# The order of two places in VectorE's program, in a fused GroupNorm, Hadamard and MLP kernel

## The reference

```python
# cut to what matters
x = x + L0(gn(x))      # L0: along the channels, pad 192 -> 256, times a 256 x 256 Hadamard matrix / 16, keep 192
x = x + L1(gn(x), ...) # L1: at each position, over its 192 channels:
#   h = x @ W1.T + b1
#   h = gelu(layernorm(h, g1, beta1))
#   h = h @ W2.T + b2
#   h = gelu(layernorm(h, g2, beta2))
#   h = h @ W3.T + b3
# gn: over 32 groups of 6 channels, mean and variance over the group's channels and all positions of an image
```

## Time and profile before

| | before |
|---|---|
| median of 3 runs | 938.48 us |
| lowest, highest | 937.85, 939.48 us |
| the profiled execution | 939.39 us |
| its span in the trace | 937.6 us |
| busy: PE, DVE, ACT, POOL | 91%, 90%, 86%, 60% of the span |
| mean granted TensorE clock | 0.976 of full speed |
| HBM read, written | 40.45 MB, 38.54 MB |

### The profile page before, as it was taken

How to read it: one execution, slowest core, us unless ns; L and a number is a source line. 1 busy time by engine, 2 the same in 40 slices (tenths; PEclk the granted TensorE clock), 3 DMA queues, 4 the chain that set the end, 5 groups by cost and what they waited for, 6 DMA issues and landing times.

```text
span 937.6 us, 22670 instructions
## 1 busy us (share of the span) xinstructions
PE 855.7 (91%) x8601; PEld 566.5 (60%) x8601; DVE 844.2 (90%) x1382; ACT 805.2 (86%) x2348; POOL 563.1 (60%) x413
## 2 busy tenths in 40 slices
PE   0668999999999999999999999999999989989997
PEld 0235666666666666666666675666666656656663
DVE  6999999999999999999999999999999989876465
ACT  2847998989999898989989898989989878978983
POOL 0314666766657566766657566766657666657660
PEclk9778999999999999999999999999999999999999
DMA  9450132332422232422422232332331111121214
GB/s 268 122 165 8 35 104 70 112 94 71 135 72 91 80 105 69 122 85 76 131 71 80 91 105 69 110 96 71 109 98 35 62 41 35 35 69 35 69 35 102
DMA packets 55420, 80.46 MB, mean 86 GB/s; under 512 B 17936, under 2 KB 18064, under 8 KB 55184
## 3 DMA queue, kind: packets, MB, share of 16 engines
q1 hardware_dynamic: 55312, 79.01, 28.0%
HBM read 40.45 MB, written 38.54 MB: 84 GB/s over the span
## 4 chain that ended last, share of the span: by engine, by line
PE 61%; DVE 27%; ACT 5%; POOL 3%; SPq 2%; issue 1%; DMA 1%; DVEq 0%; ACTq 0%
PE tm L553 14%; PE tp L565 7%; PE hl L458 7%; PE tm L548 7%; DVE z L1300 5%; PE hl L386 4%; PE hl L463 4%; PE tp L572 3%; PE tm L542 3%; DVE xs_lo L1125 3%; DVE gst L1196 3%; PE hl L391 3%; DVE X L1144 2%; DVE x_lo L1289 2%; PE hl L487 2%; POOL ge_lo L971 2%
## 5 line engine op out<-in xcount | busy, mean ns | idle before, releaser
L971 POOL TENSOR_TENSOR ge_lo<-ge,ge_hi 128x512 f16<-128x512 f32 (+1 forms) x190 | 327.1, 1732 | 84.9 <-ACT ge_hi L763 84.7
L963 POOL TENSOR_TENSOR rs<-ssq,neg_half 128x4 f32<-128x4 f32 x196 | 208.1, 1062 | 191.0 <-ACT z L733 190.2
L733 ACT ACTIVATE z<-tm 128x194 f32<-128x194 f32 x784 | 251.0, 336 | 41.6 <-PE tm L553 37.7
L1300 DVE TENSOR_TENSOR z<-tm,rs 128x768 f32<-128x768 f32 x196 | 185.9, 949 | 29.9 <-POOL rs L963 29.8
L745 ACT ACTIVATE ge<-tp,par 128x512 f32<-128x512 f32 x196 | 154.0, 785 | 39.5 <-PE tp L565 38.1
L733 ACT ACTIVATION_READ_ACCUMULATOR z<-tm 128x1 f32 x784 | 166.7, 213 | 0.0
L763 ACT ACTIVATE ge_hi<-ge 128x512 f16<-128x512 f32 (+1 forms) x190 | 160.4, 851 | 4.2
L565 PE MATMUL tp<-cst,z 128*128 128x128 f32 x784 | 123.9, 281 | 16.7 <-DVE z L1300 15.1
L565 PEld LDWEIGHTS tp<-cst,z 128*128 128x128 f32 x784 | 85.1, 142 | 42.8 <-DVE z L1300 32.2
L553 PE MATMUL tm<-w_hi,ge_hi 128*128 128x192 f16 x392 | 98.6, 251 | 0.0
L553 PE MATMUL tm<-w_hi,ge_lo 128*128 128x192 f16 x392 | 97.6, 249 | 0.0
(11 more groups left out here) (196 smaller groups left out, 2123.1 us busy)
## 6 DMA issues: line engine op xcount, KB each, us to landing
X<-x SPq DMA_DIRECT2D x48, 512.0 KB, 4.2
out<-X SPq DMA_DIRECT2D x48, 512.0 KB, 3.2
X<-x SPq DMA_DIRECT2D x96, 128.0 KB, 4.1
out<-X SPq DMA_DIRECT2D x96, 128.0 KB, 3.2
X<-weights SPq DMA_DIRECT2D x1, 1024.0 KB, 7.4
XL<-x SPq DMA_DIRECT2D x16, 32.0 KB, 3.2
XL<-x SPq DMA_DIRECT2D x32, 8.0 KB, 2.8
out<-left_ab SPq DMA_DIRECT2D x2, 256.0 KB, 3.6
```

The source lines that it names most:

```text
L733: last = nc.scalar.activation(z[n][:, 2 * h + k, i * TW:(i + 1) * TW], tm[h][:, i, k * TW:(k + 1) * TW], ACT.Square, scale=float(C) ** -0. ...
L963: nc.gpsimd.tensor_tensor(rs[n][:, 2 * h:2 * h + 2, :], ssq[n][:, 2 * h:2 * h + 2, :], neg_half[0:TT, 0:4].rearrange("p (i k) -> p i k", i=2),
L971: nc.gpsimd.tensor_tensor(ge_lo[n][:, g % 2, PART[h], :], ge[n][:, PART[h], :], ge_hi[n][:, g % 2, PART[h], :], ALU.subtract).then_inc(s_g ...
L1300: nc.vector.tensor_tensor(z[n][:, 2 * h:2 * h + 2, 0:2 * C].rearrange("p k (i o) -> p i k o", i=2), tm[h][:, :, 0:2 * TW].rearrange("p i ( ...
```

## The change

Two places in VectorE's lists are written in another order. No instruction is added or removed, and the lists of the other engines stay as they are.

```diff
@@ def step_left(g):
                 x1_split_lo(unit_at(g + 1), 2)
+                final_c(g - 2)
                 scaled_lo(h_unit(g + 1), 2)
-                final_c(g - 2)
                 normalise(g - 1, 1, 1)
@@ def step_norm(g):
+                gn_stats(chain_at(g), 1)
+                gn_stats(chain_at(g), 2)
+                gn_stats(chain_at(g), 3)
                 residual(h_unit(g), 0)
-                gn_stats(chain_at(g), 1)
                 stats_part(g, 0)
-                gn_stats(chain_at(g), 2)
                 stats_part(g, 1)
                 stats_part(g, 2)
-                gn_stats(chain_at(g), 3)
                 normalise(g, 0, 0)
```

## The result

| | before | after |
|---|---|---|
| median of 4 runs | 938.85 us | 912.32 us |
| lowest, highest | 937.85, 939.48 | 910.97, 913.21 |
| ratio, 95% interval | | 0.9717 (0.970 to 0.9734) |
| the profiled execution, its span | 939.39, 937.6 | 913.21, 911.4 |
| a regular period of three steps | 52.62 | 50.69 |

The change takes 26.5 us off the medians and 26.2 off the spans.

The account below looks back on a forecast made before the run. TensorE was taken as the bound, except where VectorE makes it wait. 7.5 + 11.6 + 2.7 = 21.8 us off the profiled 939.39 gave 917.6, off the median 916.7; forecast 917.0, range 914 to 927.

Parts of the forecast that it names:

- The gap at L565: TensorE's wait for L1300 ahead of the transposes: its 0.58 us goes, 0.02 to spare, worth 13 x 0.58 = 7.5 us.
- the upper bound of 0.86 us: In step_norm, the most L1199 could stand until GpSimd's L963 ends; the prediction took 0 instead.
- rival 1: GpSimd's L963 holds VectorE as ge_lo does, L1199 waits, TensorE meets its bank 0.88 us late; 928.1 us, chance 0.07.
- nobody waits at L403: TensorE's matmuls reusing the bank of L1144: cost put at 0.01 us; TensorE idle there would prove the prediction wrong.
- L1220's wait: TensorE's wait for L1220, 0.24 us in a period: L1220 starts earlier, at 415.04, and 2.7 us go.
- Rival 3: GpSimd's second ge_lo gets in ahead of L1125, TensorE's gap grows from 0.58 to 2.27; 946.2 us, chance 0.03.
- rival 4: Collisions move into the next step: L1121 meets a ge_lo, TensorE pays 3.2 us a period; 958.3 us, chance 0.04.
- rival 2: The 0.02 us margin at the transposes turns negative and one gap stays; 924.2 us, chance 0.09.
- idle time named, as forecast: TensorE's waits for L1205 (11.6 us), L1300 (7.5) and L1220 (2.7) all go, 21.8 us in sum.
- Together 1.71 us, and 52.6 less 1.71 is 50.9: TensorE's named waits of 0.58, 0.89 and 0.24 in one period; without them its own work of 50.9 us is left.
- one irregular period: A period outside the regular 13 that might lose its stall too; the range allowed a little more gain for it.
- the wait at L337: TensorE's wait for L1205 ahead of the group sums: its 0.89 us goes, worth 13 x 0.89 = 11.6 us.

Follow-up runs that it names:

- e1: The changed kernel with the final sum L1341 put back behind L1125, the three small operations still ahead of the residual; 919.49 us, ratio 0.9793.
- e7: The changed kernel with only L1205 moved, behind L1121, so that TensorE waits longer at L337; 960.70 us, ratio 1.0236.
- e4: The changed kernel with only L1205 moved, behind L1169, which gives TensorE a wait at L337 again; 926.64 us, ratio 0.986.
- e2_final_only: The kernel before with only the final sum L1341 moved ahead of L1125, the three small operations left behind the residual; 937.22 us, ratio 0.998.
- e6: The changed kernel with only L1220 and L1224 moved behind the next two operations (L1125, L1300); 921.69 us, ratio 0.9813.
- e3: The kernel before with only L1196 moved ahead of the residual, L1199, L1205 and the final sum left in place; 935.53 us, one run.

## Why the prediction was right in kind and too small in size

**Right.** L1125 ends where it ended, and L1341 lies inside its stall: 1.05 long, where 1.06 was forecast. The gap at L565 went, although the margin was worked out at 0.02 us. The three small operations take 0.16, but for the L1196 of step 41; the upper bound of 0.86 us for them (rival 1) is refuted by e1. By the rule that the prediction cites for rival 1 (the Trainium skill, SBUF — State Buffer, Who interferes with whom: the second of the two to issue blocks fully) they would have blocked inside the L963, and they don't; the measurement decides. L1144 follows L1205 by 0.08, and nobody waits at L403. L1220's wait went with the rest. VectorE waits ahead of L1333, though for 0.62 us and not 0.9, for TensorE was faster than I had it. Rival 3 (GpSimd's second ge_lo overtakes) and rival 4 (new collisions in the next step) did not come, nor did rival 2.

**Wrong: the size of the sum.** The span fell by 26.2, and the parts are these:

| part | us |
|---|---|
| idle time named, as forecast (11.6 + 7.5 + 2.7) | 21.8 |
| the same 13 periods by starts: 13 x 1.93 = 25.1 | +3.3 |
| two clock falls, 1.21 each on top of the waits | +2.4 |
| start of the program, ahead of any changed step | -1.4 |
| sum | 26.1 |

The first step that failed is "Together 1.71 us, and 52.6 less 1.71 is 50.9". The measured period is 50.69. I took the idle time that a row names as the wait's whole price. At L458 0.24 us were named and 0.41 paid; at L565 0.58 and 0.60 (e1's period less the changed kernel's); at L337 0.89, and 0.92 is what is left of the 1.93. The busy time of 50.88 in the earlier trace rows seemed to confirm the 50.9, but the same 531 instructions are busy for 50.69 in the changed kernel: the last matmul ahead of a wait is booked beyond the point at which the next one would have started, so busy time and idle time were both read from the same wrong place. The 11 waits at L458 were also really 13: in the two periods with a clock fall TensorE came late enough that none was named, but it went there too, hidden in the fall.

The second is what the sum leaves out. The 13 periods that I called regular are nine of 52.62, two of 53.83, and the two with the waits of steps 39 and 42, 57.96 and 57.67; I had spoken of one irregular period only. The first of the two of 53.83, and the stretch inside it at half clock:

```profile
450.24:504.07 53.83, 52.36 (x530) 35.27 (x528) 51.27 (x84) 48.54 (x143) 34.58 (x26) 0.97 0.29 90
468.70:471.90 3.20, 3.20 (x27) 2.52 (x22) 3.10 (x8) 1.89 (x7) 1.20 (x1) 0.50 0.01 3
```

I had seen both periods and counted them among the 13 without asking what made them longer. By 468.7 the clock is down; the wait at L337 in this period had ended at 466.7. That the waits bring such falls is shown by e7 against the changed kernel, ten of eleven against none. Both falls of before start 1.9 us behind their wait at L337, as the 16 in the experiments do within 0.9 to 2.4; that these two went because the waits went is an inference from this. A fall takes 1.6 us (e4, e7) but only 1.21 more here, for the 0.41 of the wait at L458 lie inside it: 1.21 + 0.41 = 1.62. The 2.4 us are those of the profiled execution. The mean granted clock of 20 other executions of the kernel before lies between 0.975 and 0.981, with a median of 0.978, so most of them seem to have had fewer or shorter stretches at half clock than the profiled one with 0.976; how many is open.

The row ahead of the sum is no effect of the change. The second L425, which is ahead of the first changed step, stands at 85.04 us before and at 86.49 after, and between 82.8 and 87.8 in the experiments, whose program is the same up to there.

The range was too narrow for this on its low side. It allowed 3 us below the forecast, for one irregular period; the two terms that I had left out are 5.7.

## What to carry to other kernels

An operation that takes ten times as long as its twin may be held by another engine, as here by GpSimd; look for what runs beside it, and expect the stall to pass to the next operation of that kind if only this one is moved. Price a wait of TensorE by the distance between starts, against the same pair where nothing waits (at L337 that gives 0.96, still 0.04 above what the period shows), and a period that is longer than its neighbours by what is different in it. Removing the last waits of the bounding engine can give more than their sum, because the clock falls that follow them go too.

## What the runs showed of the hardware

- VectorE operations with two SBUF inputs are held by a ge_lo of GpSimd (128 x 512 or 128 x 1024, two SBUF inputs) until 0.14 to 0.20 us before its booked end: in the changed kernel's trace 25 of them start inside one, more than 0.25 us ahead of its end, and all are held. In the same trace 216 VectorE operations that read at most one tensor from SBUF start inside a ge_lo, as far ahead of its end, and none is longer than elsewhere. Two-input ones are not held by GpSimd's power operation on 128 x 4: 125 start inside an L963, 84 of them in its first 0.9 us, none longer than elsewhere. Whether it is the kind of operation or its four columns that makes it harmless was not tried. The other way round GpSimd waits: in the same trace L963 and L956 are booked as 1.19 to 1.99 us instead of 1.01 where an L1121, L1125, L1289 or L1293 is under way.
- An L1199 that starts 0.01 us behind a ge_lo (357.39 in e2_final_only) is already held, 2.14 us.
- A fall of TensorE's clock cost 1.6 us in e4 and e7, and 1.2 in the kernel before and in e2_final_only, where it swallows the 0.41 of the wait at L458. Waits of 0.6 us in each period brought none in 11 periods (e1, e6), of 0.87 one (e4), of 1.1 five (e2), of 2.11 ten (e7); the kernel before, with 0.89 beside 0.58 and 0.24, had two, and e3, with 0.69 beside the same, none. Each of these counts is from one trace. In e7 the distance from the wait's end to the fall grows from 1.0 us to 2.4 over nine periods in a row, the tenth has no fall, and in the next it is 0.9. So the place of the wait against something that runs on by itself may decide which period has one; no run varied it.
